# Another order of the small work in a software-pipelined attention loop, on one core of Trainium2

## The reference, cut to what matters

```
x = x + attention(layernorm(x))          # x: 8 x 1024 x 128, 8 heads of width 16
x = x + mixture_of_experts(layernorm(x)) # 8 experts, two chosen for each token

attention(inputs):
    xn = layernorm(inputs) * gamma + beta
    q, k, v = xn @ Wq + bq, xn @ Wk + bk, xn @ Wv + bv   # per head, 16 x 16 weights
    p = positions @ Wp
    score = ((q + u) @ k^T + rel_shift((q + v) @ p^T)) / sqrt(128)
    return (softmax(score) @ v) @ Wo + bo
router(x):
    h = gelu(layernorm(x @ Wr1 + br1) * scale + bias)
    choose the top 2 of softmax(h @ Wr2 + br2)
```

## Time and profile before

| what | value |
|---|---|
| time, median of 3 runs | 1769.05 us (1768.02 to 1770.16) |
| the profiled execution | 1768.02 us |
| its span | 1766.4 us |
| TensorE / VectorE / ScalarE / GpSimd busy | 1576.1 / 1432.4 / 1089.7 / 1156.7 us |
| mean granted clock of TensorE | 0.946 |

### The profile page before, as it was taken

The page is one execution under the profiler, slowest core; times in us unless marked ns, Lnnn a source line. Parts: engine busy times, 40 slices in busy tenths (PEclk is TensorE's granted clock), DMA queues, the critical chain, the costliest instruction groups (busy, mean ns, idle before and its releaser), DMA issues. The chain is left out here.

```text
span 1766.4 us, 50630 instructions
## 1 busy us (share of the span) xinstructions
PE 1576.1 (89%) x12534; PEld 1235.8 (70%) x12535; DVE 1432.4 (81%) x5423; ACT 1089.7 (62%) x2143; POOL 1156.7 (65%) x2139
## 2 busy tenths in 40 slices
PE   2699999999999999999999999999930999999997
PEld 1466776677677677667767667766720899999997
DVE  3479989998998898899899889889943677777775
ACT  2136676666767667666676766766710666676665
POOL 4149759858856865975885686597553366666655
PEclk8569999999999999999999999999965999999999
DMA  4534733733644463373364446337361233333333
GB/s 161 168 103 102 184 93 101 185 104 108 158 111 130 108 181 89 99 187 103 105 167 107 129 109 182 87 108 179 96 191 57 43 50 53 48 52 51 50 53 42
DMA packets 140439, 195.85 MB, mean 111 GB/s; under 512 B 27976, under 2 KB 102616, under 8 KB 140192
## 3 DMA queue, kind: packets, MB, share of 16 engines
q1 hardware_dynamic: 92608, 130.86, 27.0%
q0 software_dynamic: 47584, 62.19, 17.6%
HBM read 108.24 MB, written 75.27 MB: 104 GB/s over the span
## 5 line engine op out<-in xcount | busy, mean ns | idle before, releaser
L1008 DVE CUSTOM_DVE_ANT_0 junk<-pA,lmask 128x512 bf16<-128x512 f32 x1056 | 691.5, 682 | 106.8 <-PE pA L620 57.3
L921 ACT ACTIVATE prob<-pB 128x512 f32<-128x512 f32 x384 | 229.5, 598 | 189.9 <-PE pB L639 114.6
L1487 POOL DMA_INDIRECT out<-yb,dst x144 | 232.9, 1617 | 163.4 <-ACT yb L1561 87.2
L618 PE MATMUL pA<-K,QL 96*128 96x512 f32 (+3 forms) x792 | 286.2, 363 | 1.6 <-DVE acc L1008 1.6
L641 PE MATMUL pB<-QL,K 97*128 97x512 f32 (+3 forms) x768 | 281.3, 366 | 0.0
L639 PE MATMUL pB<-QU,K 97*128 97x512 f32 (+3 forms) x640 | 264.7, 414 | 0.9
L657 PE MATMUL pC<-prob,vext 128*32 128x256 f32 x3088 | 221.2, 387 | 26.7 <-POOL prob L523 26.7
L620 PE MATMUL pA<-K,QU 96*128 96x512 f32 (+3 forms) x660 | 233.7, 355 | 4.0 <-DVE acc L1008 3.8
L923 ACT ACTIVATE prob<-pB 128x512 f32<-128x512 f32 x384 | 227.8, 593 | 0.4
L523 POOL TENSOR_TENSOR prob<-prob,upper_diag 128x128 f32<-128x128 f32 x384 | 190.8, 497 | 32.3
L476 POOL DMA_INDIRECT routed_rows<-rows_r,idx x159 | 165.1, 1038 | 49.3 <-issue 26.5
(11 more groups left out here) (305 smaller groups left out, 3696.1 us busy)
## 6 DMA issues: line engine op xcount, KB each, us to landing
QL<-split_operands SPq DMA_DIRECT2D x67, 256.0 KB, 3.4
QU<-split_operands SPq DMA_DIRECT2D x67, 256.0 KB, 3.9
K<-split_operands SPq DMA_DIRECT2D x67, 256.0 KB, 4.6
xg<-routed_rows SPq DMA_DIRECT2D x76, 132.0 KB
QL<-split_operands SPq DMA_DIRECT2D x67, 128.0 KB, 3.4
QU<-split_operands SPq DMA_DIRECT2D x67, 128.0 KB, 3.7
K<-split_operands SPq DMA_DIRECT2D x67, 128.0 KB, 3.8
split_operands<-c_h POOLq DMA_DIRECT2D x16, 512.0 KB, 7.3
```

What stands on the lines that cost most here:

```text
L618: mm = pe.matmul(dst[:, 0:low], QL[0:KROWS, s, q], K[0:KROWS, s, k0:k0 + low], start=True, stop=True)
L921: act.activation(p[:, 0:HALF], pB[:, 0:HALF], ACT.Exp, scale=SCALE).then_inc(p_exp, 1)
L1008: v.tensor_tensor_reduce(junk[:, n % S1_BUFS, :], pA[n % S1_BUFS][:, :], lmask[:, at:at + HALF], 1.0, -3.0e38, ALU.add, ALU.max, acc[:, s, ...
L1487: po.indirect_dma_start(dram["out"], bass.IndirectOffsetOnAxis(dst[k][:, a:a + 1], 0), yb[k][:, a, :], None, compute_op=ALU.add).then_inc( ...
```

## The change

The tables get other places. The projections 2 and 3 (queries) move from head 7 to head 0 of the next round, 4 and 5 from head 0 to heads 1 and 2, 0 and 1 into head 7; only 0 and 1 are computed two batches ahead now, so that two query projections leave the code ahead of the loop. The first scatter leaves (0, 2), and the last two stand at (2, 1) and (2, 2). The position steps 0 to 5 and the stores move back by up to two units, the exchange of rows (`swap`) from head 1 to head 2 of SyncE's queue. Rows 6 and 7 go to `pM`. Contexts 0, 1 and 6, the hidden product of the router and the extra scores (`super`) move ahead by one to three units, the first normalization product from (0, 3) to (0, 1). The placement of TensorE's loop head at slot 0 of a fetch block is left out, and so is one wait of GpSimd for `out 1`. Three normalizations on VectorE take a form with two per-partition scalars in place of one with a broadcast second tensor.

Unchanged lines are left out:

```diff
-def batches(nc, eng, head=None):
-    return nc.Fori(0, B, engines=[eng.engine], hint_back_edge=True, head_slot=None if head is None else {eng.engine: head})
+def batches(nc, eng):
+    return nc.Fori(0, B, engines=[eng.engine], hint_back_edge=True)
...
-                "row 3": ((2, 1),), "context 1": ((2, 4),), "row 4": ((3, 1),), "rows 0": ((3, 3),), "rows 1": ((3, 5),), "context 2": ((3, 7),),
-                "row 5": ((4, 1),), "hidden": ((4, 3), (4, 5)), "context 3": ((4, 7),), "fold": ((5, 3),), "context 4": ((5, 5),), "logits": ((6, 0),),
-                "context 5": ((6, 3),), "ranks": ((6, 7),), "row 8": ((7, 2),), "context 6": ((7, 5),)}
-        W_AT = {"row 2": ((1, 1),), "context 0": ((1, 3),), "values 0": ((4, 5), (4, 7)), "row 6": ((5, 1),), "values 1": ((5, 5), (5, 7)),
-                "row 7": ((6, 1),), "super": ((6, 3), (6, 5))}
+                "row 3": ((2, 1),), "context 1": ((2, 3),), "row 4": ((3, 1),), "rows 0": ((3, 3),), "rows 1": ((3, 5),),
+                "context 2": ((3, 7),), "row 5": ((4, 1),), "hidden": ((4, 2), (4, 3)), "context 3": ((4, 7),), "row 6": ((5, 1),), "fold": ((5, 3),),
+                "context 4": ((5, 5),), "logits": ((6, 0),), "row 7": ((6, 1),), "context 5": ((6, 3),), "ranks": ((6, 7),), "row 8": ((7, 2),),
+                "context 6": ((7, 3),)}
+        W_AT = {"row 2": ((1, 1),), "context 0": ((1, 2),), "values 0": ((4, 5), (4, 7)), "values 1": ((5, 5), (5, 7)), "super": ((6, 0), (6, 2))}
+        ACT_OUT = {"turn 0": (1, 1), "turn 1": (1, 4), "rows 0": (3, 4), "rows 1": (3, 6), "values 0": (4, 8), "fold": (5, 4), "values 1": (5, 8)}
-        ACT_OUT = {"turn 0": (1, 1), "turn 1": (1, 4), "rows 0": (3, 4), "rows 1": (3, 6), "values 0": (4, 8), "fold": (5, 4), "values 1": (5, 8)}
-        DVE_OUT = {"row 1": (0, 2), "context 7": (0, 4), "row 2": (1, 2), "context 0": (1, 4), "out 0": (1, 6), "out 1": (2, 0), "row 3": (2, 2),
-                   "context 1": (2, 5), "row 4": (3, 2), "context 2": (3, 8), "row 5": (4, 2), "hidden": (4, 6), "context 3": (4, 8), "row 6": (5, 2),
-                   "context 4": (5, 6), "logits": (6, 1), "row 7": (6, 2), "context 5": (6, 4), "super": (6, 6), "ranks": PLACES_AT[0], "row 8": (7, 3),
-                   "context 6": (7, 6)}
-        PROJECT_AT = {4: ((0, 0), (0, 2)), 5: ((0, 5), (0, 7)), 6: ((2, 0), (2, 2)), 7: ((2, 5), (2, 7)),
-                      0: ((6, 7),), 1: ((7, 0),), 2: ((7, 2), (7, 3)), 3: ((7, 5), (7, 7))}
-        PROJECT_OUT = {4: (0, 4), 5: (0, 8), 6: (2, 4), 7: (2, 8), 0: (6, 8), 1: (7, 1), 2: (7, 4), 3: (7, 8)}
-        EARLY = 4
+        DVE_OUT = {"row 1": (0, 2), "context 7": (0, 4), "out 0": (1, 6), "row 2": (1, 2), "context 0": (1, 3), "out 1": (2, 0), "row 3": (2, 2),
+                   "context 1": (2, 4), "row 4": (3, 2), "context 2": (3, 8), "row 5": (4, 2), "hidden": (4, 4), "context 3": (4, 8), "row 6": (5, 2),
+                   "context 4": (5, 6), "logits": (6, 1), "row 7": (6, 2), "context 5": (6, 4), "super": (6, 4), "ranks": PLACES_AT[0], "row 8": (7, 3),
+                   "context 6": (7, 4)}
+        PROJECT_AT = {2: ((0, 0), (0, 2)), 3: ((0, 5), (0, 7)), 4: ((1, 3), (1, 5)), 5: ((1, 7), (2, 0)), 6: ((2, 2), (2, 3)), 7: ((2, 5), (2, 7)),
+                      0: ((7, 3),), 1: ((7, 5),)}
+        PROJECT_OUT = {2: (0, 4), 3: (0, 8), 4: (1, 6), 5: (2, 1), 6: (2, 4), 7: (2, 8), 0: (7, 4), 1: (7, 6)}
-        HIGH_AT = {(0, 1): 0, (1, 6): 1, (2, 6): 2, (3, 1): 3, (3, 6): 5, (3, 8): 6}
-        LOW_AT = {(1, 2): 0, (2, 3): 1, (2, 7): 2, (3, 2): 3, (3, 6): 4, (4, 1): 5, (4, 3): 6, (4, 4): 7}
-        POSITIONS_AT = ((2, 1), (2, 2), (2, 4), (2, 5), (2, 6), (2, 8), (5, 4), (5, 6))
-        NORMALIZE_AT = (3, 4, 5, 6, 7)
-        LN_AT = ((5, 3), (5, 4), (5, 6), (5, 8), (6, 1), (6, 2), (6, 3), (6, 5))
-        RSTD_AT = ((3, 2), (3, 4), (3, 6), (3, 7), (4, 0), (4, 1), (4, 2))
+        HIGH_AT = {(1, 5): 0, (1, 8): 1, (2, 6): 2, (3, 1): 3, (3, 6): 5, (3, 8): 6}
+        LOW_AT = {(2, 3): 0, (2, 5): 1, (2, 7): 2, (3, 2): 3, (3, 6): 4, (4, 1): 5, (4, 3): 6, (4, 4): 7}
+        POSITIONS_AT = ((2, 2), (2, 4), (2, 5), (2, 6), (2, 8), (3, 1), (5, 4), (5, 6))
+        NORMALIZE_AT = (1, 4, 5, 6, 7)
+        LN_AT = ((5, 3), (5, 4), (5, 6), (5, 8), (6, 2), (6, 5), (6, 7), (7, 0))
+        RSTD_AT = ((3, 3), (3, 5), (3, 7), (3, 8), (4, 0), (4, 1), (4, 2))
-        SCATTER_AT = ((7, 6), (0, 2), (0, 3), (0, 4), (0, 5), (0, 6), (0, 8), (1, 0), (1, 2), (1, 3), (1, 4), (1, 5), (1, 6), (1, 7), (1, 8), (2, 0))
+        SCATTER_AT = ((7, 6), (0, 3), (0, 4), (0, 5), (0, 6), (0, 8), (1, 0), (1, 2), (1, 3), (1, 4), (1, 5), (1, 6), (1, 7), (1, 8), (2, 1), (2, 2))
...
-        STORE_AT = {(3, 1): ("c", 0), (3, 3): ("c", 1), (3, 5): ("k", 0), (4, 5): ("gl", 0), (4, 6): ("gu", 0)}
+        STORE_AT = {(3, 2): ("c", 0), (3, 4): ("c", 1), (3, 6): ("k", 0), (4, 5): ("gl", 0), (4, 6): ("gu", 0)}
...
-                    if h == 1:
+                    if h == 2:
-                    if h == 2:
-                    if f"row {h + 1}" in W_AT:
-                        sp.wait_ge(w_done, w_at(b, f"row {h + 1}") + 1)
+                    if h + 1 == 2:
+                        sp.wait_ge(w_done, w_at(b, "row 2") + 1)
...
-                        if not isinstance(nb, int):
-                            po.wait_ge(m_ready, m_at(nb - 1, "out 1") + 1)
...
-            for j in range(EARLY):
+            for j in range(2):
...
-                    pe.wait_ge(e_done, (b + 1) * E_N + E_AT[5])
+                    pe.wait_ge(e_done, (b + 1) * E_N + E_AT[3])
...
-            with batches(nc, pe, 0) as b:
+            with batches(nc, pe) as b:
...
-                                if (j, places.index((h, u))) == (6, 0):
+                                if (j, places.index((h, u))) == (4, 0):
-                                project(b + (2 if j < EARLY else 1), j, places.index((h, u)), len(places))
+                                project(b + (1 if j > 1 else 2), j, places.index((h, u)), len(places))
...
-            pe.wait_ge(e_done, (B + 1) * E_N + E_AT[EARLY - 1])
+            pe.wait_ge(e_done, (B + 1) * E_N + E_AT[1])
...
-            for j in range(EARLY):
+            for j in range(2):
...
-                                evacuate(b + (2 if j < EARLY else 1), j)
+                                evacuate(b + (1 if j > 1 else 2), j)
...
-                v.scalar_tensor_tensor(xn[:, t, :], xt[:, t, :], mv[:, t, 0:1], rs[:, 2, t:t + 1].to_broadcast([P, E]), ALU.subtract, ALU.mult).then_inc(ln, 1)
+                v.tensor_scalar(xn[:, t, :], xt[:, t, :], mv[:, t, 0:1], rs[:, 2, t:t + 1], ALU.subtract, ALU.mult).then_inc(ln, 1)
...
-                    v.scalar_tensor_tensor(rows[:, t, 0:E], xres[:, t, :], mv_r[:, t, 0:1], rs_r[:, t:t + 1].to_broadcast([P, E]), ALU.subtract, ALU.mult).then_inc(r_ln, 1)
+                    v.tensor_scalar(rows[:, t, 0:E], xres[:, t, :], mv_r[:, t, 0:1], rs_r[:, t:t + 1], ALU.subtract, ALU.mult).then_inc(r_ln, 1)
...
-                    v.scalar_tensor_tensor(hr[:, t, :], hr[:, t, :], mv_h[:, t, 0:1], rs_h[:, t:t + 1].to_broadcast([P, RH]), ALU.subtract, ALU.mult).then_inc(r_hid, 1)
+                    v.tensor_scalar(hr[:, t, :], hr[:, t, :], mv_h[:, t, 0:1], rs_h[:, t:t + 1], ALU.subtract, ALU.mult).then_inc(r_hid, 1)
```

## The result

| what | before | after |
|---|---|---|
| time, median of the runs taken together | 1768.60 us (1768.02 to 1770.16) | 1840.63 us (1836.13 to 1841.25) |
| span of the profiled execution | 1766.4 us | 1834.4 us |
| mean granted clock | 0.946 | 0.922 |

The ratio is 1.0399, with a 95% interval of 1.0384 to 1.0416: slower by 4.0%, 72 us, where 5 us were forecast. The profiled execution took 1836.0 us.

The account below looks back on a forecast made before the run. GpSimd was taken to bound heads 0 to 3, TensorE, with VectorE close behind, the rest. +1.1 us a round, +8.8 in eight, less 3.1 once, on 1768.0 gave 1773.7, given as 1774 us; range 1769 to 1782.

Parts of the forecast that it names:

- the loop head: TensorE's loop start, no longer placed at slot 0: taken as nothing, with one 4.6 us landing a round at most.
- Head 0: Without the scatter in (0,2) GpSimd leads by 1.4 us; unit (0,8) falls from 4.37 to 2.65, 1.7 us gained.
- The cover: Work moved into head 1 and the start of head 2 lies inside TensorE's wait for GpSimd and costs nothing.
- Head 3: Late rotation steps delay TensorE at (3,2) by 1.75 us a round; two waits for VectorE go, 0.7 back.
- the sign set for it: TensorE's wait for a rotation step at (3,2): 2 to 3 us a round expected; under 1 us, rival A is right.
- rival A: Faster: GpSimd's lead is 2.3 us, so the delay at (3,2) is 0.4 for 1.75; 1762.9 us, chance 0.27.
- (4,2): Router's hidden product waits for VectorE's copy of row 5 in that unit: 0.7 us lost, bounds 0 and 1.0.
- Rival B: No change: losses at (4,2) and (7,3) are half, VectorE having run ahead; 1766 to 1769 us, chance 0.16.
- Head 5: Bias over the hidden rows two units sooner ends TensorE's 0.94 us wait: 0.95 back, bounds 0 and 1.2.
- Head 7: Four halves leaving give 0.97 us back, the wait at (7,3) loses 1.3; heads 6 and 7 lose 0.3 net.
- Rival C: Slower: the new normalization form holds GpSimd ahead of the sixth rotation step, 1.2 us a round; 1783 us, chance 0.08.
- Rival D: Slower: TensorE's unplaced loop start costs at most a 4.6 us landing a round, 37 us; a third gives 1785; chance 0.07.

## Why the prediction was wrong

Two steps failed, and both put a cost at nothing: the clock behind a hold, and the loop head.

*Time before and views.* "The granted clock is 1.00 through a round ..., so the clock costs nothing there" rested on two stretches of one round. It holds for all of that round and not for the loop: in five of the eight rounds of that very trace the mean is 0.958 to 0.988. With it, every hold was priced as a wait only. This is one of the two steps that failed: the hold of 1.45 us in (7,3), booked as 1.3, was worth 3.9 when it was taken out.

*Head 0, right.* (0,8) went from 4.45 to 2.64 us, 1.8 where 1.7 was foreseen.

*Heads 1 and 2.* The cover held nearly: TensorE waits 0.64 us in (1,3), and head 1 is 0.46 longer; head 2 is 1.20 shorter. The exchange of rows was hidden: no masks wait for it.

*Head 3, right in its net, wrong in its parts.* Heads 0 to 3 without the round's start come to -1.64 + 0.46 - 1.20 + 3.44 = +1.06 us against 1.75 - 0.7 = 1.05. But the agreement is luck, a balance of two errors: 2.4 us were gained in heads 0 to 2, where 1.05 were foreseen, and 3.4 lost behind them, where it was 2.1. The wait for a rotation step is 0.91 and not 2 to 3 us, a hold of 1.12 for VectorE stands ahead of it, which I had not foreseen (I had VectorE catching up, not held by the moved fifth step), and with both holds and the half clock (3,2) is 2.4 us longer. By the sign set for it, a wait under 1 us, rival A should have been right; it was not, since the wait is one of three parts of what the late step costs.

*(4,2), right:* 0.6 us of wait, head 4 0.87 longer against 0.7. Rival B, half of the losses here and in (7,3), is out with it.

*Head 5, wrong:* the wait for the hidden rows did not go (1.03 for 0.94 us; head 5 +0.10 against -0.95). The rows that TensorE waits for are VectorE's second four, still at (5,2), behind row maxima that TensorE's own first pass feeds. From 641.78 to 647.46 us in the trace before, where they end, VectorE shows no idle time. A bias that leaves its queue sooner therefore gained nothing, and with the rows a unit earlier the maxima came late in their place (0.94 us again). The new form made it 0.1 longer: for these 64 elements it takes 305 ns by the median, the old 273.

*Head 7, wait right, price wrong:* 1.45 us for 1.3, but heads 6 and 7 lost 3.9 us and not 0.3, the 3.6 more for the clock and for pieces that now stand in (7,3). Moving pieces out of (7,0) and (7,2) was booked as 0.97 us gained; it also took work away ahead of the hold. The two runs with a piece moved suggest that this goes with the fall; they do not show it.

*The form.* It costs and gives nothing that can be told (0.5 us between the two runs). Its rows in the profile after, and the old form for 64 elements in the profile before, minimum, median and maximum in ns:

```profile
L983 DVE TENSOR_SCALAR xn<-xt,mv,rs x80: 328/342/1378, 15.3 to 1332.8; 128x128 f32<-128x128 f32 x80
...
L1101 DVE TENSOR_SCALAR hr<-hr,mv_h,rs_h x72: 296/305/479, 203.0 to 1390.4; 128x64 f32<-128x64 f32 x72
...
L1105 DVE SCALAR_TENSOR_TENSOR hr<-hr,mv_h,rs_h x72: 272/273/406, 203.7 to 1320.6; 128x64 f32<-128x64 f32 x72
```

For 128 elements it takes 342 for 348, not the 286 taken, which was the row of an instruction with one per-partition scalar and not two. Rival C is out. The rule of the Trainium skill cited there (VectorE: DVE Perf Modes, The perf-mode tier table) has this form take two elements a cycle. The trace agrees with it in the rate: from 64 to 128 elements the new form takes 37 ns more and the old one 75. What the prediction left out is the part that does not depend on the length, 268 ns in the new form and 198 in the old by the same medians; at these sizes it takes the gain back.

*Before the loop, right:* the first pass starts at 71.77 for 73.75, 1.98 us earlier against 1.9, and waits for its operand's landing, as the bound said. From the last exponential of the loop to the end nothing changed (486.4 us for 486.9).

*The loop head, the other step that failed, and the largest term:* "I take nothing, since the prefetch of the branch stays" stands against 4.0 us a round. Rival D named the place and the kind and gave it 0.07; its third of a landing, 1.5 us, is near the 1.8 to 2.2 us of idle time, and it too had no clock behind it. That head 7 showed no idle time in the profile before said nothing: there the head was placed. "The prefetch of the branch stays" was no reason: it stayed, and the idle time came. The Trainium skill (Runtime: NRT & Kernel Launch, Instruction fetch mechanics) says that a taken branch whose target isn't in the engine's instruction buffer has to be fetched before execution goes on; the 21 starts of a round without slot 0, in the changed kernel and the two runs on the kernel before, fit it, with 1.6 to 3.4 us of idle time and a packet of instructions just ahead of each first matmul. Why slot 0 spares it no run shows.

*The sum.* A round: 4.03 - 0 at its start, 3.92 - 0.3 in heads 6 and 7, 0.10 + 0.95 in head 5, 0.87 - 0.7 in head 4 are 8.9 us over my 1.1, which makes the 10.0 measured. From the first exponential (103.79 before, 101.18 after) to the last (1279.47, 1347.97) the loop is 71.1 us longer in the eight rounds; the first and the last round lose less (5.0 and 6.3 us).

What stays open: what ahead of a hold brings the fall. Equal holds in the same kernel differ from round to round, and undoing the steps in heads 2 and 3 changed the count in (7,3) from 7 to 3 of 8.

## What to carry to other kernels

Read the granted clock behind every hold of TensorE, in several rounds, before a wait is priced: here the removal of a hold of 1.45 us gave back 3.9 us a round. A change that leaves a hold as it is can still bring a fall behind it: in (5,3) a hold of 0.94 us had no fall behind it in one kernel and six in eight rounds in another. Small matmuls in front of a hold may help; two runs point that way, and it is worth a try and not a rule. A placement of a loop head, once in the program, is a term of its own: taking it out cost 36 us at seven back edges, and that the trace shows no idle time there is its effect.

## What was not expected of the hardware

- Behind idle time of 1.8 us and more at a round's start the mean granted clock of the next 6 us was 0.50 to 0.72 in each of seven rounds (0.50 is the level of 1.2 GHz); behind 1.50 us with half a query product ahead of it, it was 1.00 in all eight.
- TensorE's idle time at the back edge without slot 0: 1.8 to 2.2 us in the changed kernel, 2.0 to 3.4 in the kernel before (1.6 to 3.3 with slot 104). With slot 0: none. The packets of 16384 bytes on the instruction queue are 94 with slot 0, 99 or 100 without.
- A hold of 0.94 us in (5,3) had no fall behind it in the kernel before and six in eight rounds in the run with the hidden rows a unit earlier, where it stood behind one of 0.19 us in (5,2).
- Beside a 128x512 product of GpSimd and the 128x1024 select behind it, a pair of 128x128 normalizations of VectorE took 2.42 us (new form) and 2.54 us (old form), against some 0.7 alone.
